# Moving GpSimd's additions of a pair's probability blocks to the head of the next step, in a fused two-layer attention and mixture-of-experts kernel

## What is computed

```
a = q k^T / 8, masked where query < key;  a = softmax(a);  y = a v
```

## Time and profile before

| | us |
|---|---|
| three runs | 1552.97, 1553.49, 1562.78 |
| median of them | 1553.49 |
| the profiled execution's own time | 1558.71 |
| its span, first to last instruction | 1557.0 |
| TensorE (PE) busy | 1333.0 (86%) |
| PE weight load busy | 805.6 (52%) |
| VectorE (DVE) busy | 960.1 (62%) |
| ScalarE (ACT) busy | 863.6 (55%) |
| GpSimd (POOL) busy | 604.2 (39%) |
| mean granted clock of TensorE | 0.94 of full |

### The profile page before, as it was taken

One profiled execution on the slowest core, in us unless ns is written; L12 is line 12 of the kernel. 1 busy time (PEld: TensorE's weight loads), 2 busy tenths in 40 slices (PEclk: granted clock), 3 DMA queues, 4 the chain that ended last, 5 costly groups with the idle time before them and its releaser, 6 DMA issues.

```text
span 1557.0 us, 28423 instructions
## 1 busy us (share of the span) xinstructions
PE 1333.0 (86%) x9302; PEld 805.6 (52%) x9302; DVE 960.1 (62%) x3308; ACT 863.6 (55%) x1679; POOL 604.2 (39%) x783
## 2 busy tenths in 40 slices
PE   3777898998899889998999899979888886988982
PEld 1233445554455445544554455545555554877872
DVE  3566655666666666766666656564665563675784
ACT  3765665656565656565566565745443453554563
POOL 1000332233243424332533254325344455556675
PEclk8879999999999999999999999989999998999997
DMA  8060990000000000000000000000102001142322
GB/s 316 1 240 1 9 4 1 1 8 8 1 13 10 8 1 15 8 8 1 15 8 8 1 15 1 8 1 24 45 8 78 4 8 35 39 112 59 111 82 87
DMA packets 65454, 54.67 MB, mean 35 GB/s; under 512 B 41016, under 2 KB 51648, under 8 KB 65056
## 3 DMA queue, kind: packets, MB, share of 16 engines
q1 hardware_dynamic: 60768, 43.48, 14.3%
q0 software_dynamic: 4544, 9.38, 1.8%
HBM read 21.03 MB, written 31.81 MB: 34 GB/s over the span
## 4 chain that ended last, share of the span: by engine, by line
PE 64%; DVE 21%; ACT 8%; issue 3%; another core or an unknown queue 1%; POOL 1%; DMA 0%; SPq 0%; ACTq 0%; POOLq 0%; DVEq 0%
PE outs L1757 9%; PE scores L1739 9%; PE work L1679 9%; DVE scores L1233 6%; PE outs L1883 6%; PE work L1786 4%; PE outs L1962 4%; PE scores L1708 3%; ACT a_buf L943 3%; DVE a_buf L1202 3%; PE work L1769 3%; PE scores L1870 3%; DVE ra L1226 2%; ACT ra L949 2%; PE scores L1950 2%
## 5 line engine op out<-in xcount | busy, mean ns | idle before, releaser
L1233 DVE CUSTOM_DVE_ANT_0 scores<-scores,mask_qk 128x512 f32<-128x512 f32 (+3 forms) x512 | 239.0, 518 | 207.0 <-PE scores L1708 203.1
L937 ACT ACTIVATE big<-scores 128x1024 f32<-128x1024 f32 (+1 forms) x192 | 169.4, 882 | 264.4 <-PE scores L1739 262.1
L786 POOL TENSOR_SCALAR_AFFINE_SELECT big<-big 128x256 f32<-128x256 f32 x256 | 101.6, 409 | 550.0 <-ACT big L937 549.8
L943 ACT ACTIVATE a_buf<-scores 128x1024 f32<-128x1024 f32 x256 | 248.9, 1029 | 51.9 <-PE scores L1870 51.6
L1739 PE MATMUL scores<-ra 64*128 64x512 f32 (+3 forms) x1536 | 186.6, 348 | 30.1 <-ACT big L937 17.5
L802 POOL TENSOR_TENSOR big<-big 128x768 f32<-128x768 f32 x64 | 116.7, 1823 | 125.5 <-DVE parts L1268 86.1
L1757 PE MATMUL outs<-big 128*64 128x512 f32 (+3 forms) x1024 | 163.8, 465 | 0.0
L1739 PEld LDWEIGHTS scores<-ra 64*128 64x128 f32 x1536 | 122.8, 190 | 77.9 <-ACT big L937 34.7
L1226 DVE TENSOR_TENSOR ra<-work,ra 128x512 fp32r<-128x512 f32 x128 | 88.3, 690 | 120.9 <-ACT ra L949 120.8
L1883 PE MATMUL outs<-a_buf 128*16 128x512 f32 x1024 | 145.1, 642 | 1.5 <-ACT a_buf L943 1.4
L1018 ACT ACTIVATE big<-scores,b_sb 128x128 f32<-128x128 f32 x312 | 89.4, 369 | 77.9 <-PE scores L1950 37.6
(11 more groups left out here) (223 smaller groups left out, 2600.2 us busy)
## 6 DMA issues: line engine op xcount, KB each, us to landing
sorted_rows<-xrows SPq DMA_DIRECT2D x34, 520.0 KB, 6.8
qkT<-sorted_rows SPq DMA_DIRECT2D x78, 65.0 KB
a_buf<-in_w SPq DMA_DIRECT2D x2, 2048.0 KB, 8.0
a_buf<-in_x SPq DMA_DIRECT2D x8, 256.0 KB, 2.7
x_rows<-x SPq DMA_DIRECT2D x8, 256.0 KB, 2.0
ra<-x_rows SPq DMA_DIRECT2D x8, 256.0 KB
a_buf<-choice_rows SPq DMA_DIRECT2D x6, 256.0 KB, 3.9
yT<-choice_rows SPq DMA_DIRECT2D x5, 256.0 KB
```

The costliest lines, as they stand in the source:

```text
L937: activation(prob1(g, i), d[:, :, 0:256] if i == 2 else d, ACT.Exp, scale=SCALE1).then_inc(unit_free("pair", g, i), 1)
L943: activation(prob0(c)[:, i * 1024:(i + 1) * 1024], unit_wait(act, "cosine", c, i), ACT.Exp).then_inc(unit_free("cosine", c, i), 1)
L1233: return v.tensor_tensor_reduce(scores_, scores_, mask_qk[:, SEQ - width:SEQ], -1.0, 3e38, ALU.add, ALU.min, neg_max[:, qt, j:j + 1])
```

## The change

`sum_blocks(g)` leaves step g and is called at the head of the next step's program on GpSimd, ahead of that step's first two `causal` calls. There it waits for the unit of `maxima` 0 of pair g + 2 to be freed (`unit_done` of unit "max", g + 2, 0), instead of for `negmax_ready` and `parts_ready`. The waits for `sums1(g - 1)` and for the four masked blocks stay, and so do the three additions. `causal(g, 2, 0)` stays in the pair's own step. What stood behind the additions (f's `inverse_deviations` at p = 0, `second_rows`, `send_rows`) now stands directly behind `causal(g, 2, 0)`.

```diff
-            def sum_blocks(g, p, s, h):
-
-                causal(g, 2, 0)
-                if g + 1 < ALL_PAIRS:
-                    pool.wait_ge(negmax_ready, g + 2)
-                if p in (1, 3, 5) and s is not None:
-                    pool.wait_ge(parts_ready, s * GROUPS0 + p // 2 + 2)
-                if p == 7 and h is not None:
-                    pool.wait_ge(parts_ready, h * GROUPS0 + 1)
+            def sum_blocks(g):
+
+                if g + 2 < ALL_PAIRS:
+                    unit_done(pool, "max", g + 2, 0)
                 if g:
                     work_wait(pool, "sum", g - 1)
                 pool.wait_ge(prob_masked, 4 * (g + 1))
...
             for o in early_steps():
                 t, f, h, p = o.t, o.f, o.h, o.p
+                if o.pair(-1) is not None:
+                    sum_blocks(o.pair(-1))
                 if o.pair(0) is not None:
                     causal(o.g, 0, 0)
                     causal(o.g, 1, 0)
...
                 if o.pair(0) is not None:
-                    sum_blocks(o.g, p, o.s, h)
+                    causal(o.g, 2, 0)
                 if p == 0 and f is not None:
                     inverse_deviations("f0", f * 3)
```

## The result

| | before | after |
|---|---|---|
| median of 4 runs each (us) | 1553.2 | 1595.8 |
| lowest to highest | 1551.8 to 1562.8 | 1587.7 to 1607.1 |
| span of the profiled execution | 1557.0 | 1592.9 |
| mean granted clock | 0.940 | 0.928 |

The ratio is 1.0267, 95% interval 1.0203 to 1.0331: 42.5 us slower. Predicted was 30 us slower. In the changed file the touched lines stand 3 to 5 lines higher (L1202 is now L1199, L1233 is L1230, L802 is L797, L1708 is L1705, L1870 is L1867, L1856 is L1853).

The account below looks back on a forecast made before the run. Time was lost where TensorE (86% busy) waits, as VectorE and GpSimd stop each other at a shared port pair. Costs 68.1 less gains 41.8 gave +26.3, with clock 4 together +30: 1583.5 us, range 1554 to 1604.

Parts of the forecast that it names:

- Step 5's tail: Standardizing freed of additions: TensorE gains 3.1 us of wait and 1.5 us of clock in each of six passes.
- Step 3's tail: TensorE's 1.75 us wait at the next head and 1.6 us of slow matmuls go in passes 1 to 4: 13.4 us.
- Step 1's head: Additions stop four standardizing instructions: 1.55 us late in passes 0 to 5, 3.1 in pass 6, 12.4 us in all.
- Step 3's head: Additions stop the expert choice and its cast: 3.3 us late in six passes, 2.5 in pass 6, 22.3 us in all.
- Step 7's head: Additions stop the small two-operand instructions of `unit_rows`: 2.85 us late four times, 1.5 in pass 0, 12.9 us in all.
- Late sums: Additions finish too late for TensorE's `sums1` at five pairs, by 0.1 to 1.5 us: 4.4 us, bounds 0 and 8.
- Last step: Pass 7's end: pair 62's additions behind four DMA issues delay the expert tile loads, 4.5 us, bounds 0 and 5.
- The clock behind the new waits: Lower clock after TensorE's twelve new waits at steps 3 and 7: 0 to 19 us possible, 4 taken.
- Rival 3: All new waits at steps 1, 3, 6, 7 bring 1.2 GHz, step 5's low stretch stays: +50, 1604 us; chance 0.10.
- Rival 2: VectorE keeps the shared port pair and GpSimd's addition waits, so head costs nearly vanish: -20, 1533 us; chance 0.15.
- Rival 1: Heads and tails balance, costs of 45 to 55 against gains of 42: +3 to +13, about 1561 us; chance 0.18.
- queue rival: From the experiments: GpSimd's queue order costs the time, additions standing ahead of `causal` calls, DMA issues and sums; no chance given.

Follow-up runs that it names:

- e2: Kernel before with only the additions of step 3's pairs moved to the head of step 4: 1532.6 us, ratio 0.9892.
- e10: Kernel before with only the additions of step 6's pairs moved to the head of step 7: 1568.8 us, ratio 1.0096.
- e11: Kernel before with only the additions of step 0's pairs moved to the head of step 1: 1563.1 us, ratio 1.0065.
- e1: Kernel before with only the additions of step 2's pairs moved to the head of step 3: 1577.0 us, ratio 1.0161.
- e4: Changed kernel with the three additions cut to two columns per head, waits and order kept: 1511.1 us, ratio 0.9715.
- e5: Kernel before with the three additions cut to two columns per head, waits and order kept: 1514.1 us, ratio 0.9762.
- e9: Kernel before with the change made in passes 6 and 7 alone: 1570.5 us, ratio 1.012.
- e3: Kernel before with only the additions of step 5's pairs moved to the head of step 6: 1527.5 us, ratio 0.9842.
- e12: Changed kernel with a pair's three additions replaced by five fills that read nothing, together as long: 1529.4 us, ratio 0.9852.

## Why the prediction was right, and where its sum was off

The direction and the place of every cost were right; the 30 us were 12 too few. Point by point, forecast per pass against the trace:

- *Step 5's tail*: 3.1 us of wait gone, measured 4.17 - 1.02 = 3.15. Its clock gain of 1.5 came: in step 6's interval, clock below full cost at most 3.4 us a pass before (the share missing from full speed times the length) and 0.4 to 0.6 after, and the whole interval gained 3.5 us where the terms gave 2.95.
- *Step 3's tail*: the 1.75 us wait at step 4's head is gone. The clock gain beside it did not come in the changed kernel: that interval gained 1.1 to 1.4 us in passes 2 to 4, where e2, with the same pair moved alone, gained 2.3 to 5.9 in passes 1 to 4, 3.8 on average. The forecast of 3.35 holds for the part, not for the whole: the stretch at 1.2 GHz behind step 3's own wait (852.10:858.90) now lies in this interval.
- *Step 1's head*: 1.55 forecast, 1.66 to 1.71 measured. *Step 3's head*: 3.3 against 2.8 to 3.2. One reading there was wrong: the cast was not stopped by the third addition, the addition waited for it. *Step 7's head*: 2.85 against a wait of 2.71. *Step 6's head*: 1.65 against 1.42, alone 0.87.
- *Moved ahead*: put at 0. `second_rows` beside `maxima_parts` cost 0.6 us in most passes of e2, and 0.4 us in L1246 of the changed kernel (0.60 instead of 0.20 us in pass 3).
- *Late sums* 4.4: the trace shows five, 0.45, 1.51, 0.24, 1.32 and 0.17 us, 3.7 in all. *Last step* 4.5: +3.87 in the changed trace, and e10, which has pair 62 at the head, took 22.3 us from the last pair to the expert tiles against 17.7 in e11. The path was as forecast, though the wait of TensorE that shows it was 2.75 and not 5 us.
- *The clock behind the new waits*: 4 us, for the twelve at steps 3 and 7, and nothing behind steps 1 and 6. This is the term that was mis-sized. By my terms a pass of 1 to 4 was to be 1.7 us longer (1.55 + 3.3 + 1.65 + 2.85 + 0.3 - 4.6 - 3.35), four passes 6.8; they were 23.1 longer. That is 16 us more, where I had put 4 for the clock in all passes. The other passes were to give 15.0 and gave 16.5 (2.9 of which is in one interval of pass 7 that e1, e2, e4, e5 and e11 show too, at 3.2 to 4.5), the end 4.5 and gave 3.9. So the whole miss stands in passes 1 to 4, and there mostly in intervals where I had put no cost: +1.6 at step 2, behind step 1's wait; +1.6 at step 0, behind step 7's; 1.2 of step 7's 3.9 above its wait of 2.7, behind step 6's; and about 2 at step 4, whose gain shrank behind step 3's. In pass 1 the clock was full behind step 1's wait, and step 2's interval was unchanged (+0.02).

Rival 3 named this clock term, at up to 50 us; what came lies between it and the forecast. I priced a stretch well (1.6 us, rows 5; e11's two cost 1.4), but let most of them be hidden behind ScalarE's chain, and counted none behind steps 1 and 6. The other half of that rival, that the low stretch behind step 5 stays, did not come.

**The parts do not add up, and most of the gap is in the clock.** The pairs moved alone gave +23.7 (step 2), -21 (3), -26 (5), +14.7 (6), +9.0 (0), and 0 for 1, 4 and 7 in passes 0 to 5: together about zero. The whole gave +42.5. A few us of this are pairs 1 and 4 in the last passes, which no run moved alone: in e9's trace they stand at +2.5 (step 5 of pass 6) and +1.9 (step 2 of pass 7). In passes 1 to 4 the traces have every part. Take (1 - clock) x length, added over the 32 intervals, as what the clock fell short of full speed:

| passes 1 to 4, us | time against before | clock short of full |
|---|---|---|
| before | 0 | 22.0 |
| e9 (before's code here) | +0.2 | 23.9 |
| e1, step 2's pairs | +10.5 | 30.6 |
| e2, step 3's | -14.4 | 17.3 |
| e3, step 5's | -15.2 | 11.8 |
| e10, step 6's | +10.5 | 25.7 |
| e11, step 0's | +2.3 | 19.1 |
| sum of the five, against before | -6.3 | -5.5 |
| changed kernel | +23.1 | 37.8 (+15.8) |

The whole stands 29 us above the sum of its parts, and its clock shortfall 21 us above theirs. These 21 us bound what the clock can add there; that the rest of the gap follows from it is not shown, and each column is one execution per kernel. Which of two equal waits is followed by 1.2 GHz stays open; no run held everything else fixed and changed that alone.

**The lock.** What the Trainium skill states ("SBUF — State Buffer", Who interferes with whom), that a VectorE instruction with two SBUF inputs contends with a GpSimd instruction that reads SBUF and not with one that only writes it, was borne out at rows that the forecast did not have. An instruction of 32 columns waits 1.5 us for an addition, a reduction beside it does not, and fills leave two-operand work alone. So the forecast's "any SBUF-to-SBUF work" was too wide: the reduction reads and writes SBUF too. Rival 2 (VectorE keeps the pair) is refuted by step 1's head: VectorE starts 0.22 us before GpSimd and is still stopped to the end of the third addition. One of the four took 0.34 us, as each does with GpSimd idle, and the longest 1.85. Rival 1 (balance) is refuted by the time. The queue rival of the experiments is refuted by e12 through pass 6; in pass 7 the late additions and fills do cost time, as the forecast had it.

## What to carry over

Before moving GpSimd work, list what VectorE does from SBUF to SBUF beside the old place and the new one, and move only those blocks whose new place is clear; a wait on the one colliding VectorE instruction can do as much as a move. Price a new TensorE wait with the clock stretch behind it unless the trace shows other work hiding it. And measure the moved parts together, since their costs did not add. Look also at what moves ahead when a block leaves its place: `second_rows` met a two-operand instruction there.

## What the runs showed of the hardware

- In e11 the same TensorE wait of 1.84 to 1.86 us was followed by a granted clock of 0.50 in passes 0, 1 and 5 and of 1.00 in passes 2 to 4. In e9, behind waits of 1.76 and 1.77 us, the same sixteen matmuls took 4.06 us in one pass and 2.38 in the next.
- Beside GpSimd's fills a two-operand VectorE instruction kept its time (0.19 us), while a run of four tensor_scalar lost 0.8 us and a float-to-bf16 cast 0.5 us.
- A cast and an addition that started together (846.84, changed kernel): the cast kept its 0.69 us, and the addition took 1.28 instead of 0.73 us.
- A two-operand instruction of 8 columns took 0.84 instead of 0.20 us beside a GpSimd addition of 128x512 (e2). The same 0.84 us stands in e4, so step 3's interval, 0.6 us longer there, is `second_rows` and not the additions of two columns.
